# VectorE adds the bias row of K while it takes K out of PSUM

## What is computed

```python
h = _layernorm(x) * (1 + ca) + sa
Q = elu(h @ Wq + bq) + 1;  K = elu(h @ Wk + bk) + 1;  V = h @ Wv + bv
KV = einsum('nshd,nshm->nhmd', K, V);  Ksum = K.sum(axis=1)
Z = 1 / (einsum('nlhd,nhd->nlh', Q, Ksum) + 1e-6)
out = einsum('nlhd,nhmd,nlh->nlhm', Q, KV, Z) @ Wo + bo
x = h + out        # then layer norm, relu(x @ W1 + b1) @ W2, layer norm, and the second half
```

## Time and profile before

| | us |
|---|---|
| median of 3 executions | 162.9 (162.67 to 162.97) |
| the profiled execution, its own time | 163.57 |
| its span, from the first to the last instruction | 161.8 |
| granted TensorE clock, mean over the span | 1.000 |

### The profile page before, as it was taken

How to read it: one execution, slowest core, us unless ns; L and a number is a source line. 1 busy time by engine, 2 the same in 40 slices (tenths; PEclk the granted TensorE clock), 3 DMA queues, 4 the chain that set the end, 5 groups by cost and what they waited for, 6 DMA issues and landing times.

```text
span 161.8 us, 4069 instructions
## 1 busy us (share of the span) xinstructions
PE 156.2 (97%) x1151; PEld 145.2 (90%) x1151; DVE 128.1 (79%) x582; ACT 118.2 (73%) x323; POOL 105.7 (65%) x243
## 2 busy tenths in 40 slices
PE   7899998999999999999999999999999999999992
PEld 7779797899999999989999999999999999888891
DVE  3756857888897979798888889797979878888842
ACT  4356775869696969698796969696969877566562
POOL 4337278586676778777676767677876764973631
PEclk9999999999999999999999999999999999999999
DMA  4996349900010101010010101010101001010112
GB/s 129 269 299 168 109 137 396 378 4 0 0 34 4 32 0 32 4 34 2 4 32 2 32 6 32 0 32 4 34 0 32 7 0 32 0 39 0 34 34 67
DMA packets 8190, 9.95 MB, mean 62 GB/s; under 512 B 708, under 2 KB 6376, under 8 KB 8168
## 3 DMA queue, kind: packets, MB, share of 16 engines
q1 hardware_dynamic: 7872, 9.60, 18.6%
q10 hardware_dynamic: 296, 0.08, 0.2%
HBM read 7.55 MB, written 2.13 MB: 60 GB/s over the span
## 4 chain that ended last, share of the span: by engine, by line
PE 82%; DMA 7%; POOL 4%; issue 2%; DVE 2%; ACT 1%; POOLq 0%; DVEq 0%
PE bank L1190 15%; PE bank L1080 15%; PE bank L1069 8%; PE bank L1074 4%; PE bank L1162 4%; PE bank L1118 4%; PE bank L1106 4%; PE bank L1146 4%; PE bank L1297 4%; PE bank L1134 4%; PE bank L1130 3%; PE bank L1154 3%; DMA bv_row<-bv_rows_dram 3%; DMA bv_rows_dram<-bv_rows 3%; PE bank L1173 2%
## 5 line engine op out<-in xcount | busy, mean ns | idle before, releaser
L1080 PE MATMUL bank<-w,hid 128*128 128x128 f32 x240 | 31.7, 275 | 0.0
L1190 PE MATMUL bank<-x1T,w 128*128 128x256 f32 x120 | 31.0, 382 | 0.0
L1080 PEld LDWEIGHTS bank<-w,hid 128*128 128x128 f32 x240 | 29.3, 192 | 0.0
L336 ACT ACTIVATE hid<-bank,b_cols 128x256 f32<-128x256 f32 x60 | 26.0, 511 | 1.1 <-PE bank L1190 1.1
L524 POOL TENSOR_TENSOR rstd_n<-vare_n,power 128x2 f32<-128x2 f32 x30 | 23.8, 792 | 2.3
L1190 PEld LDWEIGHTS bank<-x1T,w 128*128 128x128 f32 x120 | 21.4, 190 | 2.9 <-DVE z L766 0.3
L312 ACT ACTIVATE hT<-bank,modT 128x256 f32<-128x256 f32 x16 | 9.0, 564 | 19.9 <-PE bank L1069 19.9
L520 POOL TENSOR_TENSOR vare_n<-mv_n,eps 128x2 f32<-128x2 f32 x30 | 5.9, 197 | 15.4 <-DVE mv_n L669 15.3
L281 ACT ACTIVATE n<-x_all,shift_n,rstd_n 128x128 f32<-128x128 f32 x30 | 13.1, 485 | 2.5 <-POOL shift_n L532 2.5
L675 DVE TENSOR_SCALAR ny<-bank,mv_ny,rstd_ny 128x128 f32<-128x128 f32 x32 | 11.6, 405 | 3.0 <-POOL rstd_ny L524 1.6
L675 DVE TENSOR_SCALAR n<-x,mv_n,rstd_n 128x128 f32<-128x128 f32 x28 | 8.4, 343 | 6.0 <-POOL rstd_n L524 6.0
(11 more groups left out here) (186 smaller groups left out, 453.2 us busy)
## 6 DMA issues: line engine op xcount, KB each, us to landing
gm_rows<-mod_rows_dram SPq DMA_DIRECT2D x2, 960.0 KB, 9.2
out<-out_sb SPq DMA_DIRECT2D x15, 128.0 KB, 1.8
gm_rows<-mod_rows_dram SPq DMA_DIRECT2D x1, 768.0 KB, 6.3
w<-in_w SPq DMA_DIRECT2D x1, 512.0 KB, 5.7
bv_row<-bv_rows_dram SPq DMA_DIRECT2D x1, 512.0 KB, 4.6
bv_row<-bv_rows_dram SPq DMA_DIRECT2D x1, 384.0 KB, 4.8
gm_rows<-mod_rows_dram SPq DMA_DIRECT2D x1, 384.0 KB, 3.7
x_all<-in_x SPq DMA_DIRECT2D x2, 128.0 KB, 2.8
```

The lines of the kernel that those rows point to most:

```text
L336: last = nc.scalar.activation(hid[:, f, :], bank[:, f % 2 * L:(f % 2 + 1) * L], ACT.Relu, bias=b1_cols[:, f:f + 1])
L1080: last = nc.tensor.matmul(banks[6][:, c * D:(c + 1) * D], hid[:, f, c * 128:(c + 1) * 128], w2[:, f, :], start=False, stop=(f == FF - 1 an ...
L1190: return nc.tensor.matmul(bank[:, f % 2 * L:(f % 2 + 1) * L], w1[:, f * 128:(f + 1) * 128], x1T[:, :], start=True, stop=True)
```

## The change

The bias product per sequence is gone from the K product, whose float32 products now each start and end their own sum. DVE adds the bias row instead: a new tensor_tensor reads the 128x256 of banks[4] and bias_row, broadcast over the two chunks, and writes kb in SBUF. It stands ahead of attention() in DVE's order. k_exponent and the k_sb instruction read kb and not banks[4], k_exponent waits for kb_ok, and the next K product needs kb_ok in place of k_ok. At the start, one product of 128 columns puts the bias row into banks[5]; DVE copies it to bias_row (behind second_n1(0)), and the first Q product, which writes banks[5], waits for that copy.

```diff
--- before.py
+++ after.py
@@ -88,6 +88,7 @@
         hT = [sb(f"hT{p}", [128, L]) for p in range(2)]
         exp_k = sb("exp_k", [128, NC, D])
         k_sb = sb("k_sb", [128, NC, D])
+        bias_row, kb = sb("bias_row", [128, D]), sb("kb", [128, NC, D])
         exp_q = sb("exp_q", [128, L])
         relu_q = sb("relu_q", [128, L])
         qT = sb("qT", [128, L])
@@ -131,6 +132,7 @@
 
 
         x_in = [sem(f"x_in{i}") for i in range(4)]
+        row_mm, row_ok, kb_ok = map(sem, ("row_mm", "row_ok", "kb_ok"))
         cols_loaded, kq_loaded = sem("cols_loaded"), sem("kq_loaded")
         wmod_loaded = [sem(f"wmod_loaded{i}") for i in range(2)]
         wvo_loaded, w12_loaded, mix_loaded = map(sem, ("wvo_loaded", "w12_loaded", "mix_loaded"))
@@ -318,8 +320,8 @@
                                      bias=beta1_b2[:, :]).then_inc(x1T_ok, 1)
 
             def k_exponent(s):
-                need(act, k_mm, s + 1)
-                nc.scalar.activation(exp_k[:, :, :], chunked(banks[4]), ACT.Exp, bias=neg1[:, :]).then_inc(expk_ok, 1)
+                need(act, kb_ok, s + 1)
+                nc.scalar.activation(exp_k[:, :, :], kb[:, :, :], ACT.Exp, bias=neg1[:, :]).then_inc(expk_ok, 1)
 
             def q_exponent(s):
                 need(act, q_ok, s)
@@ -856,6 +858,14 @@
                 if live(t - 3):
 
                     centred(sp_)
+                if t == 0:
+                    dve.wait_ge(row_mm, 1)
+                    nc.vector.tensor_copy(bias_row[:, :], banks[5][:, 0:D]).then_inc(row_ok, 1)
+                    dve.wait_ge(row_ok, 1)
+                if live(t):
+                    need(dve, k_mm, sa + 1)
+                    nc.vector.tensor_tensor(kb[:, :, :], chunked(banks[4]), bias_row[:, :].unsqueeze(1).broadcast_to([128, NC, D]),
+                                            ALU.add).then_inc(kb_ok, 1)
                 if live(t - 1) and not draining(t):
                     attention()
                 if t == 2:
@@ -865,7 +875,7 @@
                 if live(t):
 
                     need(dve, expk_ok, sa + 1)
-                    nc.vector.scalar_tensor_tensor(k_sb[:, :, :], exp_k[:, :, :], 1.0, chunked(banks[4]), ALU.min,
+                    nc.vector.scalar_tensor_tensor(k_sb[:, :, :], exp_k[:, :, :], 1.0, kb[:, :, :], ALU.min,
                                                    ALU.max).then_inc(k_ok, 1)
                 if t == 0:
                     second_n1(1).then_inc(n1_ok, 1)
@@ -1138,13 +1148,11 @@
             def k_product(s):
 
                 need(pe, hT_ok, s + 1)
-                need(pe, k_ok, s)
+                need(pe, kb_ok, s)
                 need(pe, tanh_ok, s - 4)
-                nc.tensor.matmul(chunked(banks[4]), ones3[:, :], bias_parts[:, :].unsqueeze(1).broadcast_to([128, NC, D]),
-                                 start=True, stop=False)
                 for c in range(NC):
                     last = nc.tensor.matmul(banks[4][:, c * D:(c + 1) * D], hT[s % 2][:, c * 128:(c + 1) * 128],
-                                            wk, start=False, stop=(c == NC - 1))
+                                            wk, start=True, stop=True)
                 last.then_inc(k_mm, 1)
 
             def q_product(s):
@@ -1198,7 +1206,9 @@
                 direct_row(1)
                 pe.wait_ge(parts, 6)
                 pe.wait_ge(const_dve, 7)
+                nc.tensor.matmul(banks[5][:, 0:D], ones3[:, :], bias_parts[:, :], start=True, stop=True).then_inc(row_mm, 1)
                 k_product(0)
+                pe.wait_ge(row_ok, 1)
                 q_product(0)
                 bv_product()
                 state_product(0)
```

## The result

The changed kernel takes 170.47 us (median of 4 executions, 170.03 to 170.67) against 162.94 us (4 executions, 162.67 to 163.06) of the kernel before beside it: ratio 1.0436, 95% interval 1.0401 to 1.047, so 7.5 us slower. The forecast was 172.2 us with a range of 168.5 to 174.8. The profiled execution has a span of 168.9 us, before 161.8: 7.1 us more.

The account below looks back on a forecast made before the run. PE was taken as full, with two chains just in time beside it: DVE to att and ACT to attT. First steps 1.7, step 3 0.8 and middle 6.8 sum to 9.3 us: 162.9 + 9.3 = 172.2 us, range 168.5 to 174.8.

Parts of the forecast that it names:

- step 15: No next sequence, so DVE reaches the add early and it ends before exp_k's turn: 0 us booked.
- A: Rival: PE sets the time and the add falls into DVE's idle fifth; 161.3 us, chance 4%.
- B: Rival: ACT makes up its delay ahead of attT and only att is late; 167.8 us, chance 10%.
- D: Rival: the small gain and a small loss cancel; 162.9 us, chance 2%.
- The add: New DVE instruction once a sequence, directly ahead of att: 0.41 us, bounds 0.30 and 0.47.
- The read from SBUF: exp_k on ACT reads SBUF in place of PSUM: 0.03 us more, bounds 0 and 0.10.
- the middle step: Steps 4 to 14: exp_k waits for the add, attT is late and PE waits; 0.62 us each, 6.8 us.
- the other effects: In the middle, att, k_sb, mixes and norms also move later, but stay under the 0.62 us of attT's delay.
- Rival C: DVE's delay brings a further wait late, say mix or k_sb: some 0.3 us more a step; 175.5 us and above, 10%.
- The start and step 3: First steps 1.7 us (bounds 1.2 and 2.6) and step 3 0.8 us (bounds 0.5 and 1.2).
- The detour through DRAM: SP's rows sent through DRAM in the first steps, which POOL waits 2.88 us for: adds nothing to the delay.
- the idle 0.41 us of PE at 26.27: PE's idle time after the first steps takes up a part of their 2.15 us delay, leaving 1.7 us.

Follow-up runs that it names:

- exp_waits: The kernel before with one more wait: exp_k also waits for att of the sequence before, with no add anywhere; 170.72 us, ratio 1.045.
- no_bias: The kernel before without the bias product of K and with nothing in its place; 163.48 us, ratio 1.0006.
- before_mix: The kernel before with only the mix moved ahead of the n3 statistics on DVE; 163.19 us, ratio 0.997.
- add_unused: The kernel before with a 128x256 add from SBUF ahead of att on DVE, its result unread, exp_k not waiting for it; 168.16 us, ratio 1.0287.

## Why the prediction was right, and where it was off

- **The sign and the mechanism** held. exp_k waits for the add in every middle step and not at step 15; PE waits for att and for attT; exp_waits shows that a late exp_k costs the step its delay, with no add at all. Rivals A, B and D are out. B had attT in time, but in after the loads of L1084 wait 2.3 us for attT in six steps. D had the loss cancel a small gain, and there is no gain. As for A, no_bias shows that PE's 0.11 us a step are worth nothing, so even a free add would not have given A. By the Trainium skill's rule that spoke for A (Perfetto Trace Analysis, Identifying the Most-Contended Engine), PE was the engine to relieve; here no_bias (1.0006) decides against it.
- **The add**, taken at 0.41 us, measured 0.411. **The read from SBUF**, taken at 0.03, measured 0.033. The Trainium skill's 0.04 (Perfetto Trace Analysis, Optimizing Scalar/DVE Operations) would have done as well.
- **The mis-sized term is the middle step:** booked 0.62 us, measured 0.39; over eleven steps 6.8 against 4.58. The signs that went with it missed as well: a step of 9.3 to 9.5 us and waits of exp_k of 0.6 us were forecast, 9.17 and 0.26 measured. The start of the add was read in a step in which DVE had lost 0.26 us ahead of att; no other step from 4 to 14 of before loses as much. The same loss made att look as if it had 0.1 us or less to spare; at t=9 the load of its transposes starts at 80.37, 0.24 us after att ends. By the rows of t=9 the same working gives 79.66 + 0.41 + 0.05 = 80.12 for exp_k, 0.38 us late, which with 0.03 for the read and less the 0.05 of slack is 0.36: 4.0 us in all. The stall, no longer hidden, makes that step 9.41 us long in after, so it adds another 0.24 to the eleven.
- **That the other effects lie under attT's delay** was right in size and incomplete as a reason. DVE's chain to mixT is about as late, because k_sb waits 0.18 us for exp_k on top of the add. The prediction had it keeping its distance from PE; it does so only while PE is itself late. Rival C is there, hidden behind the forecast's own wait, and adds no time of its own to the changed kernel.
- **The start and step 3**, booked at 2.5 us, took 2.04 against the profiled execution of before, and 2.53 against before_mix. The detour through DRAM added nothing in after, as said, where POOL waits 0.26 us for bv_row. But the prediction missed that the idle 0.41 us of PE at 26.27, which it let take up a part of the delay, was the detour's own doing in that one execution; it isn't there in before_mix and no_bias. Without it the same working gives 2.15 + 0.8 = 2.95 us, so that 2.53 lies near 2.5 is in part luck.
- **The sum:** 9.3 us were booked, 2.04 + 4.58 + 0.08 = 6.7 measured. The later load adds 0.40 to the span. The profiled execution of before lay 0.63 us above its median, that of after 0.20 above its own, which adds 0.43 to the difference of the medians: 7.5 us. The late landing, 0.49 us, is of the size of that 0.63; no trace of the other executions shows whether it is the cause.

Left open: what DVE lost its 0.26 us to at t=8. In after it lies in the same step, but between two other instructions (gated and the aggregate of z, 73.15 and 73.69, where the next step has 82.55 and 82.87). In both traces that is near the 260th instruction that DVE executes (counted without register, branch and semaphore instructions). The stall comes in step 8 of all fourteen traces. In before, exp_waits, no_bias and after it comes behind 258 or 259 instructions, whatever the length of the step, and in the same four a second one of 0.15 to 0.22 us comes behind 455 to 459, in before at t=14. So it goes with a place in DVE's program and not with a time; why it is there no run here tested.

## What to carry to other kernels

- Before a row of one step prices eleven, compare it with the same row two steps away. From step 4 on the hT starts of before are 8.78 to 8.80 us apart; the stall was hidden inside the step and showed only in the gap between two neighbours on DVE.
- A full engine is a bound only if taking work from it shortens the step. Here the loop over ACT was just as long, so the removal gave nothing, while a hand-over inserted into that loop cost about as much as it made exp_k late.
- When an edit removes a wait and the time doesn't move, look for the next wait behind it before giving up the theory: two chains that are equally late need both edits (4.2 us together, nothing alone).

## What the runs showed of the hardware

An add of 128x256 on DVE with both operands in SBUF takes 0.36 to 0.42 us alone and 0.69 or 0.70 us when it starts while POOL's out_sb, an instruction of the same shape, runs (add_unused: nine of its sixteen adds). What sets the time seems to be the end of out_sb: the add at 90.90 ends at 91.59, 0.27 us after out_sb (90.59 + 0.73), and the one at t=8, which starts 0.47 us after out_sb and not 0.31, takes 0.54 and ends 0.29 after it. With one operand in PSUM it stays at 0.36 to 0.42 us, although out_sb runs beside it there too (84.12 to 84.85 in after, the add 84.44 to 84.85). The Trainium skill (GPSIMD Engine Reference, Specifications) says that GpSimd shares its SBUF interfaces with VectorE and contends with VectorE's instructions that have two SBUF inputs; the trace agrees. k_sb, which now has two SBUF inputs, is only 11 ns dearer, as out_sb has ended when it runs.
